# Two attention layers on one core: where the score rows and value products stand in TensorE's order

## The reference, cut to what matters

```python
# layer 0
dots = jnp.einsum('bhid,bhjd->bhij', q, k) * scale
dots = jnp.where(causal_mask[None, None, :, :], -jnp.inf, dots)
attn = jax.nn.softmax(dots, axis=-1)
out = jnp.einsum('bhij,bhjd->bhid', attn, v)
# layer 1: 16 query heads, 4 key heads
qk = jnp.einsum('bhid,bhjd->bhij', q, k) * scale
qk = qk + alibi_slopes(H)[None, :, None, None] * dist[None, None, :, :]
qk = jnp.where(allowed[None, None, :, :], -1000000000.0, qk)
attn = jax.nn.softmax(qk, axis=-1)
```

## Time and profile before

| | us |
|---|---|
| median of three runs | 1095.2 |
| the profiled execution, whole | 1093.62 |
| its span, first to last instruction | 1091.9 |
| PE busy | 992.9 (91%) |
| DVE busy | 699.2 (64%) |
| ACT busy | 606.6 (56%) |
| POOL busy | 348.0 (32%) |

### The profile page before, as it was taken

How to read it: one execution, slowest core, us unless ns; L and a number is a source line. 1 busy time by engine, 2 the same in 40 slices (tenths; PEclk the granted TensorE clock), 3 DMA queues, 4 the chain that set the end, 5 groups by cost and what they waited for, 6 DMA issues and landing times. The chain is left out here.

```text
span 1091.9 us, 18023 instructions
## 1 busy us (share of the span) xinstructions
PE 992.9 (91%) x6546; PEld 518.2 (47%) x6546; DVE 699.2 (64%) x1535; ACT 606.6 (56%) x1204; POOL 348.0 (32%) x418
## 2 busy tenths in 40 slices
PE   6587999999989899978799999999999989899997
PEld 4342323333324578755333343433333334588996
DVE  2766877777753457569788777787777735235323
ACT  4334667666766433462467667777777676523221
POOL 3022122231111335341343453614233251424323
PEclk9798999999999899999899999999999999999999
DMA  7443011121000020042443140303121000000001
GB/s 261 160 145 98 16 46 59 59 60 50 11 2 1 18 71 1 8 121 89 141 107 112 52 148 16 125 2 125 34 92 37 1 2 1 1 1 20 20 1 39
DMA packets 32996, 64.20 MB, mean 59 GB/s; under 512 B 6095, under 2 KB 22367, under 8 KB 30532
## 3 DMA queue, kind: packets, MB, share of 16 engines
q1 hardware_dynamic: 31564, 58.47, 17.1%
q0 software_dynamic: 1072, 3.80, 1.0%
q10 hardware_dynamic: 272, 0.79, 0.2%
HBM read 50.45 MB, written 12.32 MB: 57 GB/s over the span
## 5 line engine op out<-in xcount | busy, mean ns | idle before, releaser
L1020 ACT ACTIVATE prob<-ps 128x512 f32<-128x512 f32 (+6 forms) x896 | 442.9, 537 | 208.8 <-PE ps L1063 201.2
L1063 PE MATMUL ps<-qop,kop 98*128 98x512 bf16 (+15 forms) x1376 | 302.6, 291 | 21.5 <-ACT prob L1020 7.9
L1049 PE MATMUL ps<-kop,qop 96*128 96x512 bf16 (+3 forms) x896 | 254.5, 358 | 37.9 <-DVE maxes L955 32.2
L1063 PEld LDWEIGHTS ps<-qop,kop 107*128 107x128 bf16 (+2 forms) x1376 | 114.5, 98 | 279.1 <-ACT prob L1020 200.8
L1090 PE MATMUL ps<-prob,vst 128*32 128x512 f32 (+4 forms) x1792 | 211.8, 544 | 3.9 <-POOL prob L892 2.6
L955 DVE CUSTOM_DVE_ANT_0 sums<-ps,tri 128x128 bf16<-128x128 f32 (+7 forms) x256 | 184.1, 755 | 47.1 <-PE ps L1049 45.8
L955 DVE CUSTOM_DVE_ANT_0 sums<-ps,table 128x960 bf16<-128x960 f32 x128 | 148.0, 1156 | 71.2 <-PE ps L1049 56.3
L892 POOL TENSOR_TENSOR prob<-prob,keep 128x384 int32<-128x384 int32 (+2 forms) x144 | 122.6, 853 | 221.7 <-ACT prob L1020 219.2
L1486 PE MATMUL ps<-xs,wffn 128*128 128x512 f32 x640 | 156.5, 400 | 3.7 <-PEq L730 2.2
L955 DVE CUSTOM_DVE_ANT_0 tri<-ps,table 128x960 bf16<-128x960 f32 x128 | 147.5, 1152 | 3.3 <-PE ps L1049 3.3
L1486 PEld LDWEIGHTS ps<-xs,wffn 128*128 128x128 f32 x640 | 120.7, 191 | 30.7 <-issue 4.2
(11 more groups left out here) (103 smaller groups left out, 687.5 us busy)
## 6 DMA issues: line engine op xcount, KB each, us to landing
table<-in_table SPq DMA_DIRECT2D x32, 464.0 KB, 4.7
qop<-q_parts SPq DMA_DIRECT2D x96, 128.0 KB, 2.7
kop<-k_parts SPq DMA_DIRECT2D x48, 128.0 KB, 2.6
kop<-k_parts SPq DMA_DIRECT2D x48, 96.0 KB
q_parts<-qop SPq DMA_DIRECT2D x8, 384.0 KB, 3.0
q_parts<-kop SPq DMA_DIRECT2D x8, 384.0 KB, 2.6
x<-in_x SPq DMA_DIRECT2D x4, 512.0 KB, 5.8
k_parts<-qop SPq DMA_DIRECT2D x4, 384.0 KB, 4.5
```

The costliest lines, as they stand in the source:

```text
L1020: nc.scalar.activation(prob[0:rows, q % 2, k % HG, lo % CH:lo % CH + hi - lo], ps[0:rows, t_bank(n, k), lo % CH:lo % CH + hi - lo], ACT.Ex ...
L1049: last = nc.tensor.matmul(ps[:, S_BANK + 2 * (k % S_SLOTS) + a // CH, a % CH:a % CH + b - a], qop[0:RD, par, h, i0:i0 + P], kop[0:RD, par, ...
L1063: return nc.tensor.matmul(ps[0:rows, bank, a % CH:a % CH + b - a], lhs, rhs, start=start, stop=True, skip_group_check=True)
```

## The change

It has four parts.

1. **Layer 0's groups** take their order from a table (`GIVEN`: how many M's stand behind each E, 12 quads of 4, for group 0 and for the others; `VALUES_BEHIND`: behind which E of quad n the V of quad n-1 stands, 4 being the place it had). "parts" comes right behind the last M of the stream.
2. **Layer 0's opening**: the finish of unit u-1 stands behind unit u, where before two units and their finishes were grouped; every turn, unit, v and the last finish count 1, and the M's count 1 each whatever their width.
3. **Layer 1, groups 1 to 7**: the M's of a quad stand together behind the second E.
4. **Layer 1, last key tile**: the E's load 128 columns of weights and not 64. The columns past the end are those of the next version of the position rows, whose order is changed so that there is one; what they give is not read.

```diff
+GIVEN = ("2211 1010 4011 0200 1020 2110 1012 2110 1100 2110 1101 0011",
+         "1110 2001 0110 2000 1102 0002 2011 0110 1210 0200 0200 0101")
+
+VALUES_BEHIND = ((4, 4, 4, 4, 1, 2, 1, 3, 4, 3, 3), (2, 4, 3, 3, 2, 2, 4, 4, 4, 4, 3))
...
 def plan(layer, group):
 
+    if layer.index == 0:
+        return plan_by_table(layer, group)
...
+    def behind(h, done, due):
+        if layer.index == 1 and late:
+            return done if h == 0 else due
+        return done + -(-(due - done) // (HG - h))
+
...
-            upto = given + -(-(due - given) // (HG - h))
+            upto = behind(h, given, due)
             steps += [("max", u, later) for u, later in stream[given:upto]]
             given = upto
-            upto = given_next + -(-(due_next - given_next) // (HG - h))
+            upto = behind(h, given_next, due_next)
...
+def plan_by_table(layer, group):
...
+    for n, (half, kt) in enumerate(quads):
+        for h in range(HG):
+            steps.append(("exp", HG * n + h, 0))
+            for unit in maxima[at:at + given[HG * n + h]]:
+                steps.append(unit)
+                at += 1
+                if at == len(stream):
+                    steps.append(("parts", 0, 1))
+            if n >= 1 and values_behind[n - 1] == h + 1:
+                steps.append(("values", n - 1, 0))
+                if quads[n - 1][0] != half:
+                    steps.append(("evict", quads[n - 1][0], 0))
+        if n == 0 and late:
+            steps += [(what, k, -1) for what, k in tail[:2]]
+        if n == 1 and late:
+            steps.append((*tail[2], -1))
...
-PE_SHARE = {"turn": 0.85, "unit": 1.72, "v": 1.72}
+PE_SHARE = ({"turn": 1, "unit": 1, "v": 1}, {"turn": 0.85, "unit": 1.72, "v": 1.72})
...
-    width = [hi - lo for _, _, lo, hi in units]
+    width = [hi - lo for _, _, lo, hi in units] if layer.index == 1 else [1] * len(units)
...
+        if layer.index == 0:
+            due = -(-work * (n + 1) // (len(units) - 2))
...
             for j in range(4):
-                one, two = units[2 * j:2 * j + 2]
-                out += [one, two, ("finish", one[1]), vs[j], ("finish", two[1])]
-            return out
+                for _, u in units[2 * j:2 * j + 2]:
+                    out += [("unit", u), ("finish", u - 1)] if u >= 1 else [("unit", u)]
+                out.append(vs[j])
+            return out if b == 0 else out + [("finish", len(self.units) - 1)]
...
-            return self.steps(1)
+            return [*self.steps(1)[:-1], ("finish", len(self.units) - 1, 1)]
...
-                     kpos[NPOS - 2:NPOS, 1:2, :].to_broadcast((2, L.key_sets, T))).then_inc(self.const_rows[buf], 16)
+                     kpos[NPOS - 2:NPOS, 0:1, :].to_broadcast((2, L.key_sets, T))).then_inc(self.const_rows[buf], 16)
...
-                    return nc.tensor.matmul(ps[0:rows, bank, a % CH:a % CH + b - a], lhs, rhs, start=start,
+                    return nc.tensor.matmul(ps[:, bank, a % CH:a % CH + b - a], lhs, rhs, start=start,
...
-                for v, a, b in ((1, 0, j0 + WIN), (2, j0 + WIN, j0 + 3 * WIN), (0, j0 + 3 * WIN, T)):
+                for v, a, b in ((0, 0, j0 + WIN), (1, j0 + WIN, j0 + 3 * WIN), (2, j0 + 3 * WIN, T)):
                     a, b = max(a, lo), min(b, hi)
                     if a < b:
-                        last = mm(a, b, kop[0:RA, par, v, j0:j0 + rows], q[:, a:b], start)
+
+                        sets = kop[0:RA, par, :, :].rearrange("p v t -> p (v t)")
+                        last = mm(a, b, sets[:, v * T + j0:v * T + j0 + P], q[:, a:b], start)
...
-    kpos = np.stack([left, -left, left * mixed], axis=1)
+    kpos = np.stack([-left, left * mixed, left], axis=1)
```

More of the change, by code:

```diff
@@ L172, in plan @@
     return steps
-PE_SHARE = {"turn": 0.85, "unit": 1.72, "v": 1.72}
+def plan_by_table(layer, group):
+    quads = quads_of(layer)
+    nq, nu = len(quads), len(units_of(layer))
+    rows_at = nq - KEY_TILES_AHEAD[0]
+    lead = nu * KEY_TILES_AHEAD[0] // nq
+    late, last = group >= 1, group == N - 1
+    given = [int(c) for quad in GIVEN[late].split() for c in quad]
+    values_behind = VALUES_BEHIND[late]
+    stream = [("max", k, 1) for k in range(lead if late else 0, nu)] if group + 1 < N else []
+    maxima = stream + ([("max", k, 2) for k in range(lead)] if group + 2 < N else [])
+    tail = [("values", nq - 1), ("evict", 1), ("norm", 1)]
+    steps, at = [], 0
+    for n, (half, kt) in enumerate(quads):
[14 more added lines that the diff above has]
+            steps.append((*tail[2], -1))
+        if n == 1 and not last:
+            steps.append(("stage", 0, 1))
+        if n >= 2 and quads[n - 2][0] != quads[n - 1][0]:
+            steps.append(("norm", quads[n - 2][0], 0))
+        if n == rows_at and stream:
+            steps.append(("rows", 0, 1))
+        first = RESIDUAL_GROUP[0]
+        if first <= group < first + 4 and n in RESIDUAL_QUADS[0]:
+            steps.append(("residual", 4 * (group - first) + RESIDUAL_QUADS[0].index(n), 0))
+    if last:
+        steps += [(what, k, 0) for what, k in tail]
+        steps = with_preparation(steps, nq)
+    return steps
+PE_SHARE = ({"turn": 1, "unit": 1, "v": 1}, {"turn": 0.85, "unit": 1.72, "v": 1.72})
 def opening_of(layer, proj):
     units = units_of(layer)
-    behind = [step if len(step) == 3 else (*step, PE_SHARE.get(step[0], 0.0)) for step in proj.beside_maxima()]
+    behind = [step if len(step) == 3 else (*step, PE_SHARE[layer.index].get(step[0], 0.0)) for step in proj.beside_maxima()]
     out = []
@@ L1058, in shifted @@
                 lo, hi = columns_of(L, half, kt)
-                j0, rows = key_tile(L, kt)
+                j0, _ = key_tile(L, kt)
                 q = qop[0:RA, par, h, :]
                 def mm(a, b, lhs, rhs, start):
-                    return nc.tensor.matmul(ps[0:rows, bank, a % CH:a % CH + b - a], lhs, rhs, start=start,
+                    return nc.tensor.matmul(ps[:, bank, a % CH:a % CH + b - a], lhs, rhs, start=start,
                                             stop=True, skip_group_check=True)
```

## The result

The changed kernel takes **1064.13 us**, the median of 4 executions (1063.19 to 1065.82). The kernel before, run beside it, takes 1094.7. The ratio is 0.972, with an interval of 0.970 to 0.974, so the change saves 30.6 us. The forecast was 29.4 and 1065.8 us.

A forecast was written before the change was run, and what follows sets the result against it. PE ends each stage, with stalls on exponentials and reductions in layer 0 and ACT's chain setting layer 1's quads. Terms -12.0 - 1.6 - 1.2 - 5.0 - 6.5 - 3.1 = -29.4 us took 1095.2 to 1065.8, 8-in-10 range 1059 to 1076.

The forecast's parts named there:

- The walk: Layer 0, groups 1 to 5, new order priced step by step: 30.6 us a group, 2.4 less, -12.0 in all.
- the three reasons it listed: Layer 0's late groups: V mid-quad in 1, 5, 6; two wide M's in quad 10; quad 11's second M last.
- Rival 6: Layer 0's table only moves stalls between quads and only layer 1's parts count: 1085.6 us, chance 0.04.
- Rivals 2 and 5: Layer 0: V's wait for masks, halving the gain (about 1072.6 us, chance 0.10) or making the kernel slower (chance 0.02).
- Group 7: Layer 0's last group, without M's: exponentials and preparation set it, so moved V's give 0 (+0.5 to -0.5) us.
- Group 6: Layer 0, no M's after quad 7; the walk is ahead up to there: -1.6 us (0 to -2).
- group 0: Layer 0's first group, DVE nearly the bound with 42 M's: -1.2 us (+1 to -3).
- The opening: Layer 0 before group 0: 4.4 us less DVE idle, first reduction 0.9 sooner; -5.0 us taken (+3.2 to -6.5).
- Layer 1's block: Layer 1, M's together behind E1: the second exponential starts sooner, 0.08 us a quad, -6.5 us (0 to -8).
- The period is ACT's chain and not PE's work: Layer 1's quads: E3 waits for ACT's exponentials, while PE's steps before it end sooner, at 1.48 us against 1.63.
- 128 columns: Layer 1's last key tile: wider weight loads save 0.24 us in each of 13 quads, -3.1 us (0 to -3.3).
- Rival 4: Layer 1's block starves DVE, M's wait and the 6.5 us are not had: 1072.3 us, chance 0.06.

The follow-up runs named there:

- e6: Changed kernel with the table's M's but every V of layer 0 at its quad's end, group 7 included: 1079.17 us, ratio 0.985 to the kernel before.
- e7: Changed kernel with the table's places of V but the M's dealt evenly as before: 1082.98 us, ratio 0.989 to the kernel before.
- e8: Changed kernel with each mask of layer 0 taken twice by POOL, same values: 1082.14 us, ratio 0.988 to the kernel before.
- e1: Changed kernel with the V's of layer 0's group 7 alone back at the quad's end: 1061.65 us, ratio 0.969 to the kernel before.
- e3: Changed kernel with the E's of layer 1's last key tile loading 64 columns of weights again: 1066.05 us, ratio 0.974 to the kernel before.

## Why the prediction was right

**Layer 0, groups 1 to 5.** The walk gave 30.6 us and the profile has 30.58. Of single quads, quad 5 was walked to 2.74 us and measured 2.68, quad 10 to 2.16 and 2.14. What the prediction didn't say is that the three reasons it listed don't add: e6 and e7 show that V in the middle and the moved M's have to be had together. I had walked only the whole order, which is why the sum came out right, and my expectations for the halves were guessed from it and wrong. Rival 6, that the table only moves stalls, is what each half alone does.

**Masks.** "V of quad 0 arrives 0.05 us after its mask" is borne out: the V's of groups 1 to 6 wait for none, and e8's 0.7 us more cost 0.70 in quad 1. Rivals 2 and 5 are out in these groups. In group 7 the prediction's own sign, "no wait of V's for POOL of over 0.2 us", fails: two of them wait 1.21 and 1.54 us.

**Group 7 is the step that failed.** The prediction put it as "V's moved within quads change what PE does while it waits: 0 (+0.5 to -0.5)". It measured +4.0 in the stage and +3.6 up to the last V, and e1 takes 3.3 to 4.1 back. The step rested on "ACT's exponentials and the preparation set it", as if PE's place in the queue were free there. The trace of the kernel before says otherwise: up to the last V PE is busy for 31.8 us of 35.9 and ACT for 22.1. The moved V's added 3.1 us to PE's idle time, 4.0 before and 7.1 after, by their own waits and by the last one, which comes of the preparation that moved along with the V of quad 10. In groups with M's the same places are paid by M's in front of them. Group 7 could have been walked like the late groups; I walked only the groups with M's.

**Group 6** (-1.7 for -1.6) was right, **group 0** gave 1.9 for 1.2 in this profile. In the five kernels with the whole new opening and both halves of the table it takes 35.7 to 37.1, and the two that reach it last (87.1 and 87.4 us) are among the three shortest, so opening and group 0 are better read together: 8.1 us for a forecast of 6.2.

**The opening** was mis-sized, -6.2 for -5.0: its 4.4 for the deal were right, and its 0.9 for the finishes is 1.7 in the same profile. "The first operand load starts about 3.2 us later. That is covered" held: in the new kernel the first M starts at 40.94 us, after a wait of 2.91 for its operand's load, and DVE, in the ternary passes, takes it up at 45.47. The first E came at 86.06 where "near 87" was expected.

**Layer 1's block** was right in the wait that it removes, and too small in its size, by 0.02 to 0.04 us in a 448-column quad. "The period is ACT's chain and not PE's work" goes too far: PE's V is part of the path. Undone alone, the block costs 7.7 us in the groups that it changes (9.0 in the medians), for a forecast of 6.5. Part of that is not the block's own: **128 columns** is worth 2.9 us without the block and 1.9 with it, since both touch the same changes between E and M. The two together give 11.5 us by the profiles, for a forecast of 9.6, and about 1.0 of that is the difference in group 0 that goes with the clock. Rival 4 is out: in the late groups DVE isn't starved and no quad lengthens.

So the sum was right partly by luck: 4.0 us lost in group 7 stood against 1.2 in the opening, 0.7 in group 0 and 1.9 in layer 1 (with the 1.0 that goes with the clock) that were underrated. With the 1.5 of the last stage this makes the 27.8 of the profiles; the 30.6 of the medians can't be taken apart by stage. e1 shows what the change gives when its one bad place is put back: 1061.65 us, 33 less than before.

## What to carry to other kernels

When steps are moved on a queue in program order, walk every kind of stage in which the new order is used, and look up the busy times of each before calling a place in the queue free. A step that waits at the head of the queue delays all that stand behind it, and a step that is tied to a moved one (here the preparation to V) moves with it. Two edits to one order must be walked together and tested both apart and together, for here each half gave a late group nothing and both gave it 2.4 us. Where an order depends on what fills a gap (here the M's between E's), give the stage without the filler an order of its own.

## What the runs showed that was not expected

**The clock behind group 7.** In nine of the ten profiles the granted clock falls to 0.50 (the 1.2 GHz level) for some 7 or 10 us near the last E of group 7, where PE has fewer matmuls to run. The stage view of e1, in stretches of 20 us from that E on, and then the same of e6:

```profile
336.10:356.10 20.00, 15.63 (x83) 12.01 (x81) 10.02 (x18) 9.64 (x19) 5.65 (x7) 0.83 0.08 24
356.10:376.10 20.00, 18.93 (x112) 16.65 (x111) 11.25 (x21) 5.48 (x9) 7.68 (x7) 1.00 0.28 96
```

```profile
356.50:376.50 20.00, 15.61 (x93) 12.40 (x91) 11.14 (x19) 9.66 (x19) 6.91 (x8) 1.00 0.08 24
376.50:396.50 20.00, 18.92 (x119) 16.86 (x118) 10.13 (x20) 5.57 (x10) 6.41 (x6) 1.00 0.29 96
```

Group 7 takes as long in both (31.4 us to its last E), and from there to layer 1 e6 takes 179.4 us and e1 181.5. The difference is there in full (2.2 us) at the same instruction some 14 us behind the last E, and stays. Why e6 keeps the clock there isn't shown: its group 7 is written as in e1, and only what stands before it differs.

**The same opening, two microseconds apart.** With identical steps up to group 0, seven kernels reach the first E between 85.3 and 87.4 us, and the spread is there by the first reduction. So a term of 1 to 2 us in such an opening is read from DVE's idle time, which repeats to 0.7 us, and not from the time at which it ends.

**Half the columns of weights load slower:** 108 ns for 64 against 97 for 128, and M's and E's beside them start 0.1 us later, above.
